# Last stage of an attention and mixture-of-experts kernel: eight residual products issued before the expert rows return, and POOL's row additions moved to four later batches

## The reference

```
out = out + comb[:, e:e + 1] * oe          # for each expert e
return h + out.reshape(B, S, H)            # h is the residual
...
x = _layernorm(x + _L0_ffn_ref(x, ...), axis=-1)
```

## Time and profile before

| what | value |
|---|---|
| time, median of 3 runs | 367.7 us (365.55 to 368.96) |
| profiled execution | 366.52 us, span 364.7 us |
| mean granted TensorE clock | 0.949 |
| TensorE busy | 315.9 us, 87% of the span |
| VectorE, ScalarE, POOL busy | 255.6, 238.4, 210.9 us |
| first load of rows issued | 331.16 us from the span's start |
| last normalising write of ScalarE starts | 356.6 us |

### The profile page before, as it was taken

One profiled execution on the slowest core, in us unless ns is written; L12 is line 12 of the kernel. 1 busy time (PEld: TensorE's weight loads), 2 busy tenths in 40 slices (PEclk: granted clock), 3 DMA queues, 4 the chain that ended last, 5 costly groups with the idle time before them and its releaser, 6 DMA issues.

```text
span 364.7 us, 8735 instructions
## 1 busy us (share of the span) xinstructions
PE 315.9 (87%) x2052; PEld 273.7 (75%) x2052; DVE 255.6 (70%) x1031; ACT 238.4 (65%) x559; POOL 210.9 (58%) x251
## 2 busy tenths in 40 slices
PE   4859598749989989998999899899999999993970
PEld 3749487637878878987887788688888888872860
DVE  3385977797878869886988888866776666630660
ACT  2758655446776686776777677577777877750471
POOL 0394877848347656765587777676444443342760
PEclk9998788968999999999999999999999999996996
DMA  8266841143113121112112211332211111005931
GB/s 256 78 202 202 257 158 45 46 98 109 47 30 89 38 54 49 56 32 62 51 48 62 58 54 60 92 100 71 54 46 51 45 41 35 18 18 170 348 118 58
DMA packets 27872, 31.97 MB, mean 88 GB/s; under 512 B 4769, under 2 KB 21413, under 8 KB 27824
## 3 DMA queue, kind: packets, MB, share of 16 engines
q1 hardware_dynamic: 23504, 22.88, 20.8%
q0 software_dynamic: 4320, 8.53, 7.1%
HBM read 20.16 MB, written 11.68 MB: 87 GB/s over the span
## 4 chain that ended last, share of the span: by engine, by line
PE 67%; DVE 11%; issue 6%; ACT 5%; POOL 4%; DMA 3%; SPq 0%; POOLq 0%; ACTq 0%; DVEq 0%
PE bank L547 17%; PE bank L496 9%; PE bank L498 8%; PE bank L497 8%; PE bank L533 7%; POOL expert_rows L1331 3%; PE bank L449 2%; PE bank L557 2%; PE bank L697 2%; PE bank L433 2%; PE bank L691 2%; PE bank L410 2%; PE bank L411 1%; DMA w_raw<-weights 1%; PE bank L440 1%
## 5 line engine op out<-in xcount | busy, mean ns | idle before, releaser
L1340 POOL DMA_INDIRECT moe_rows<-ysb,xrow x71 | 70.4, 992 | 90.7 <-ACT ysb L768 84.6
L547 PE MATMUL bank<-wd,hidT 128*128 x568 | 76.4, 277 | 4.8 <-ACT t L775 3.9
L1331 POOL DMA_INDIRECT expert_rows<-rows,place x64 | 63.0, 985 | 20.7 <-issue 13.8
L547 PEld LDWEIGHTS bank<-wd,hidT 128*128 128x128 f32 x568 | 68.9, 192 | 7.6 <-issue 7.5
L496 PE MATMUL bank<-w_hi,t_hi 128*128 x142 | 63.1, 444 | 6.6 <-DVE t_lo L1179 3.1
L498 PE MATMUL bank<-w_hi,t_lo 128*128 x142 | 56.5, 398 | 0.0
L497 PE MATMUL bank<-w_lo,t_hi 128*128 x142 | 56.3, 397 | 0.0
L781 ACT ACTIVATE th<-bank 128x512 f32<-128x512 f32 x71 | 42.5, 599 | 16.6 <-PE bank L498 16.5
L1186 DVE SCALAR_TENSOR_TENSOR hid<-th,bank 128x512 f32<-128x512 f32 x71 | 48.3, 681 | 3.7 <-ACT th L781 3.7
L1190 DVE TENSOR_TENSOR hid<-hid,bank 128x512 f32<-128x512 f32 x71 | 48.8, 687 | 2.4
L1177 DVE CAST t_hi<-t 128x128 fp32r<-128x128 f32 x71 | 17.6, 248 | 45.7 <-ACT t L775 45.3
(11 more groups left out here) (158 smaller groups left out, 570.7 us busy)
## 6 DMA issues: line engine op xcount, KB each, us to landing
xrow<-expert_rows SPq DMA_DIRECT2D x71, 66.0 KB, 1.8
w_raw<-weights SPq DMA_DIRECT2D x16, 256.0 KB, 4.1
w_lo<-moe_rows SPq DMA_DIRECT2D x16, 256.0 KB, 5.5
xT<-xt SPq DMA_DIRECT2D x8, 256.0 KB, 4.3
wd<-weights SPq DMA_DIRECT2D x4, 512.0 KB, 8.7
out<-xs SPq DMA_DIRECT2D x16, 128.0 KB, 1.7
xs<-x SPq DMA_DIRECT2D x3, 512.0 KB, 7.1
moe_rows<-ysb,xrow POOLq DMA_INDIRECT x71, 2.3
```

The source lines that it names most:

```text
L547: last = mm(ps_y, hidT[i % 2][:, c * P:(c + 1) * P], wd[:, bass.ds(w + c * P, P)], start=(c == 0), stop=(c == NC - 1))
L1331: G.indirect_dma_start(out=expert_rows[:, :], out_offset=bass.IndirectOffsetOnAxis(ap=place[:, i, k:k + 1], axis=0), in_=rows[:, i, k, :], ...
L1340: G.indirect_dma_start(out=moe_rows[:, :], out_offset=bass.IndirectOffsetOnAxis(ap=xrow[i % XR][:, C_DST:C_DST + 1].bitcast(I32), axis=0), ...
```

## The change

TensorE now issues the residual's products of batches 0 to 7 in one go, behind the two waits and before any wait for rows. Then batches 0 to 7 each wait for their load and take two products, result 1 and result 0, whether odd or even. Batches 8 to 15 stay as they were: odd ones with three products, even ones with two, POOL's sum among them. The additions on POOL are those of batches 8, 10, 12 and 14 alone, so the wait counts for `yadd_done` change.

POOL's loop has eight steps. Step `g` takes the power of group `g` first (after the wait for the variance, and from group 2 on for ScalarE's reads of group `g - 2`), and in steps 0 to 3 it then waits for the load of batch `8 + 2g` and adds.

```diff
             pe.wait_ge(sm["res_done"], 2 * TOKEN_TILES)
             pe.wait_ge(sm["ysb_done"], MOE_TILES)
+            for b in range(8):
+                mm(ps_z(b), ident, xs[:, b, :, :], start=True, stop=False)
             for b in range(B):
                 if b >= 8:
                     pe.wait_ge(sm["o_done"], NT * (b - 7))
-                mm(ps_z(b), ident, xs[:, b, :, :], start=True, stop=False)
-                if b % 2:
+                    mm(ps_z(b), ident, xs[:, b, :, :], start=True, stop=False)
+                if b < 8 or b % 2:
                     pe.wait_ge(y_in[b], 16)
                     mm(ps_z(b), ident, yin[b][:, :, 1, :], start=False, stop=False)
                 else:
-                    pe.wait_ge(sm["yadd_done"], b // 2 + 1)
+                    pe.wait_ge(sm["yadd_done"], b // 2 - 3)
                 mm(ps_z(b), ident, yin[b][:, :, 0, :], start=False, stop=True).then_inc(sm["z_done"], 1)
...
-            for g in range(GROUPS + 2):
-                if g < GROUPS:
-                    pool.wait_ge(y_in[2 * g], 16)
-                    G.tensor_tensor(yin[2 * g][:, :, 0, :], yin[2 * g][:, :, 0, :], yin[2 * g][:, :, 1, :], ALU.add
+            for g in range(GROUPS):
+                pool.wait_ge(sm["var3_done"], g + 1)
+                if g >= 2:
+                    pool.wait_ge(sm["o_done"], GT * (g - 1))
+                G.tensor_tensor(rs3[g % 2][:, :], var3[g % 2][:, :], mhalf[:, 0:GT], ALU.pow
+                                ).then_inc(sm["rs3_done"], 1)
+                if g < GROUPS // 2:
+                    b = 8 + 2 * g
+                    pool.wait_ge(y_in[b], 16)
+                    G.tensor_tensor(yin[b][:, :, 0, :], yin[b][:, :, 0, :], yin[b][:, :, 1, :], ALU.add
                                     ).then_inc(sm["yadd_done"], 1)
-                if g >= 2:
-                    pool.wait_ge(sm["var3_done"], g - 1)
-                    if g >= 4:
-                        pool.wait_ge(sm["o_done"], GT * (g - 3))
-                    G.tensor_tensor(rs3[g % 2][:, :], var3[g % 2][:, :], mhalf[:, 0:GT], ALU.pow
-                                    ).then_inc(sm["rs3_done"], 1)
```

## The result

The changed kernel takes 364.59 us (median of 20 runs, 363.18 to 366.19), the kernel before 367.48 (20 runs). The ratio is 0.992, 95% interval 0.9909 to 0.9932: 2.9 us less, between 2.5 and 3.3. The profiled execution took 364.64 us with a span of 362.8. The forecast was 2.7 less. All ratios here compare fast executions alone; on the chips of the experiments up to a third of a kernel's executions ran slower and stay out of them.

The account below looks back on a forecast made before the run. After the last expert tile, TensorE's count of products, not row landings, was taken as the bound. Terms 0.75 + 1.3 + 1.7 - 1.0 = 2.7 us off the 367.7 median gave 365.0, range 362.9 to 367.2.

Parts of the forecast that it names:

- Products ahead, at no cost: Last stage, TensorE: eight residual products from 328.80 take 3.4 us and end before the first rows land at 333.8.
- No add before the first product: TensorE's first product after rows starts at batch 0's landing, 333.85, not after POOL's add at 334.61: 0.75 us.
- the 0.75: Gain in us claimed for batch 0 no longer waiting for POOL's add before TensorE's first product after rows.
- 36 products against 39: TensorE's products after the first landing, 36, against 39 after POOL's first add: 1.3 us gained at 0.43 each.
- Waiting for landings and restarts, 1.0: Loss on TensorE in us: 0.5 + 0.4 waiting for rows of batches 2 and 3, 0.1 for a restart.
- the 16.5 of the sum: TensorE's time from 333.85 on after the change: 15.5 us of products, 0.5 + 0.4 of waiting, 0.1 restart.
- The clock, no fall: TensorE's clock stays at 2.4 GHz through the wait for rows, saving the 1.7 us that products at 1.2 GHz cost.
- POOL's wait for batch 8 (C, taken as 0): POOL's add waiting for batch 8's rows delays batch 10's bank: 0.3 us slack; as rival, gain 1.8 to 2.3, chance 0.12.
- rival A: TensorE's clock is at 1.2 GHz when rows come, returning at 337.8: gain 1.8 us, 365.9, chance 0.18.

Follow-up runs that it names:

- POOL's half: Kernel before with POOL adding only for batches 8, 10, 12, 14 and three products in place for batches 0 to 7: ratio 1.002, last stage 29.13 us.
- the warm kernel: Kernel before with seven further products, later overwritten, in front of the last stage: ratio 0.999 to before, last stage 26.91 us.
- The first half alone: Changed kernel's eight residual products ahead, but POOL adding for all eight even batches as before: ratios to before 0.994 and 0.995, last stage 25.98 and 25.52 us.

## Why the prediction was right, step by step

- **Products ahead, at no cost:** right. Eight at 0.43 are 3.4 us (3.69 to the end of the last record), and TensorE then stood 1.33 us before the first rows.
- **No add before the first product:** right; the load releases it 5.02 us after the stage's first product, as forecast (5.05). But the 0.75 is not a gain of POOL's half as such: alone with it the stage was longer.
- **36 products against 39:** right as the count that sets the end (no adds, 40 products: 0.8 to 1.5 more for four). But it is the sum of two moves that cancel in part. With the residual ahead and the old adds there are 32, and TensorE waits for POOL in their place.
- **Waiting for landings and restarts, 1.0:** too small; it was 1.65 in the first profile. The waits are 0.92 before batch 2 and 0.20 before batch 3, against 0.9 for both, and 0.1 at batch 10. Batch 2 could start 0.5 later after the stage's first product than the loads of before said, batch 3 0.3 later. The restart, put at 0.1 once, came four times: behind the waits for batches 0, 2, 3 and 10 the next product starts 0.53 to 0.54 us later, not 0.43. From the first product of rows to the end of the last it is so 17.2 us against the 16.5 of the sum, and that is the difference between 2.7 and the 2.13 of this pair of profiles. The second profile, with less waiting, has 2.56, the third 1.91.
- **The clock, no fall:** right in all three profiles of the changed kernel, with waits of 1.3 to 1.5 us. Its worth was put at 1.7 within the sum; the warm kernel before gave 1.35. The expectation for it had part of the 1.7 turn into waiting for rows and adds.
- **POOL's wait for batch 8 (C, taken as 0):** near the edge, as said: 0.1, 0 and 0.7 us by starts of products in three profiles, in the order of POOL's add for batch 8, which its rows released 12.3, 11.8 and 12.5 us after the first product. The price of its steps lacked one term, the shift held for 0.55 us by POOL's add. It stayed small because TensorE was late itself: it was due at batch 10 15.5 us after its first product in the first profile, not 15.0.
- **The argument against rival A was too strong.** It said that after dense products no fall was to be expected. The first half alone, in its second run, has one: dense products, a wait of 2.2 us, and then

```profile
351.40:354.20 2.80, 0.67 (x3) 0.62 (x4) 0.00 (x0) 0.00 (x0) 0.72 (x1) 1.00 1.01 316
354.50:357.60 3.10, 3.10 (x8) 2.44 (x8) 2.23 (x13) 0.00 (x0) 1.67 (x3) 0.50 1.00 364
357.90:369.00 11.10, 11.10 (x53) 9.60 (x51) 10.55 (x60) 8.43 (x23) 9.68 (x12) 1.00 0.79 287
```

  The clock fell as the work came back. The Trainium skill (TensorE: Matmul & The Clock Gate, HAM oscillation) describes this for short bursts of matmuls between waits for DMA, where the next burst starts cold. The trace agrees with it here. But the first half's first profile and the warm kernel stood 2.11 and 2.23 us behind dense products and kept 1.00, so which of such waits ends cold is open. The fall cost this stage nothing that shows: 25.52 us against 25.98 without it, with TensorE waiting for POOL's adds around it.

The whole time moved by 2.9, the stage by 1.9 to 2.6 in single profiles against one profile of before, whose execution (366.52) was 1 us under its median. So the forecast's 2.7 lies closer to the whole time than to the stage it was worked out for, and that closeness is in part luck. Whether a typical execution of before loses the rest in this stage is open: there is one profile of it.

## What to carry to other kernels

Work that needs nothing from a transfer belongs in front of the wait for it, if its results have a place to stay: here it both leaves the path and keeps TensorE's clock up, and packing two batches to a bank took what could go ahead from 8 batches to 15. When a change has two halves, test each: the second can cancel a saving that the first would have had (here products on POOL against products on TensorE). And before trusting a chain that runs through another engine, take that engine's wait out once; level paths hide behind each other.

## What the runs showed of the hardware

The shift on VectorE, which reads two operands from SBUF, does not finish while POOL's add runs. At 128x4 it takes 0.13 us alone; in the changed kernel it takes 0.68 when it starts inside POOL's add, and ends with it. POOL and VectorE of the changed kernel at group 1:

```profile
343.03 0.72 POOL L1446 TENSOR_TENSOR w_lo<-w_lo 128x256 f32<-128x256 f32 x1
...
343.09 0.68 DVE L1302 SCALAR_TENSOR_TENSOR shift<-mv,rs 128x4 f32<-128x4 f32 x1 [1.48 <-POOL rs L1441]
```

With the adds one step later the group 1 shift starts further into the add and is shorter by as much, and both end together again (353.16 and 353.17):

```profile
352.43 0.73 POOL L1446 TENSOR_TENSOR w_lo<-w_lo 128x256 f32<-128x256 f32 x1 [0.21 <-DMA w_lo<-moe_rows]
```

```profile
352.56 0.61 DVE L1302 SCALAR_TENSOR_TENSOR shift<-mv,rs 128x4 f32<-128x4 f32 x1
```

Over all 13 profiles 30 shifts start inside an add. They take 0.23 to 0.69 us, the longer the earlier in the add they start, and end 0.01 to 0.03 us after it; the other 74 take 0.13 to 0.17. Since the power releases the shift and the add follows the power at once on POOL, the two start together by construction.

The variance (L1322 in the first half alone), which reads one tile, is held too. It takes 0.15 to 0.17 us, but 0.69 and 0.57 in the two cases, one in each profile of that kernel, where it starts early in an add:

```profile
350.40 0.72 POOL L1439 TENSOR_TENSOR w_lo<-w_lo 128x256 f32<-128x256 f32 x1 [2.34 <-DMA w_lo<-moe_rows]
```

```profile
350.47 0.69 DVE L1322 TENSOR_SCALAR var<-mv 128x4 f32<-128x4 f32 x1
```

The statistics, which read PSUM, are not: in the kernel before a pair starts at 340.37 inside POOL's add of 340.24 to 340.96 and takes 0.49 us, as it does elsewhere. The Trainium skill (GPSIMD Engine Reference, Specifications) says that POOL shares its SBUF interfaces with VectorE, in contention with VectorE instructions that have two SBUF inputs or are in a 2-port perf mode. The trace agrees for the shift; whether the variance is in such a mode no run shows. The short instruction pays the whole rest of the long one, 0.55 us for the shift here. In the kernel before, the shift came just after the add had ended, and nothing of this was to be seen.
